# Recurrence of a test-time-training layer: corrections in two sets of matmuls, query products moved, no filler

## The chip, the cores and the metric

The kernel runs on one core of one Trainium2 chip. The metric is the device time of one execution in microseconds (us): the median of the runs, from the start of the execution to its end. Beside it stands one execution taken by the profiler, whose span runs from the first to the last instruction. A core has five engines with a queue each: PE (TensorE, matmuls into PSUM), DVE (VectorE), ACT (ScalarE), POOL (GpSimd) and SP (SyncE, which issues the DMAs here). They wait for each other by semaphores alone.

## The reference

Two residual layers follow each other on an image of 4 x 256 x 32 x 32. The second, a convolution with a spatial descriptor, is not touched by the change. The first is a layer whose state, a matrix W1 (32 x 32) and a bias b1 for each of 8 heads and 4 images, is trained while it reads: the 1024 tokens go through in 64 chunks of 16, and each chunk takes one gradient step. Its core:

```python
def _ln_l2_bwd(Z, tgt, g, b):
    D = Z.shape[-1]
    mu = Z.mean(-1, keepdims=True)
    var = ((Z - mu) ** 2).mean(-1, keepdims=True)
    std = jnp.sqrt(var + EPS_IN)
    xh = (Z - mu) / std
    gxh = (g * xh + b - tgt) * g
    return (D * gxh - gxh.sum(-1, keepdims=True) - xh * (gxh * xh).sum(-1, keepdims=True)) / (D * std)
...
def step(carry, inp):
    W1c, b1c = carry
    xq, xk, xv, et = inp
    Z1 = xk @ W1c + b1c
    grad = _ln_l2_bwd(Z1, xv - xk, g, bb)
    Attn1 = jnp.tril(xq @ xk.swapaxes(-1, -2))
    b1_bar = b1c - jnp.tril(et) @ grad
    Z1_bar = xq @ W1c - et * Attn1 @ grad + b1_bar
    last_eta = et[..., -1, :, None]
    W1n = W1c - (last_eta * xk).swapaxes(-1, -2) @ grad
    b1n = b1c - (last_eta * grad).sum(-2, keepdims=True)
    return ((W1n, b1n), xq + _ln(Z1_bar, g, bb, EPS_IN))
```

## The kernel before

**Stages.** Everything is float32. A first block normalises the input, a second makes queries, keys and values with their rotation (to about 160 us). The third block holds the scan over the 64 chunks (first start of a chunk's work on ACT at 168.3 us, last at 450.5 us), and behind it the output projection and the second layer. The change touches the scan alone.

**A chunk of the scan.** The 128 partitions are 4 groups of 32 rows; a group holds two heads with 16 tokens each, and the 4 images lie side by side in the free dimension, so a tile of one chunk is 128 x 128. Two buffers alternate by the chunk's parity `p`, with `o = 1 - p`.

- PE's `base` (L1157 to L1178) makes Z of the next chunk with the state as it stands, and in the same matmuls the products of keys with keys and of queries with keys: 16 matmuls of 64 rows (L1169), then one with the identity for the bias (L1175). All go to one PSUM bank, `ZB[p]`: per image 32 columns of Z and 32 of products. A float32 matmul is two records in the trace, so 16 matmuls are 32 records.
- That state lacks the gradient of the chunk just before. So the gradient `GL` of chunk c-1 is put into chunk c by a correction: `grads(ZW, ZB[p], o, 1)` (L1180 to L1189, matmuls at L1184) multiplies the masked products `AM` by `GL` and adds to Z in the same bank, 16 matmuls of 32 x 32.
- ACT squares the corrected Z (L1573). DVE sums the squares (L1317), sums and centres Z (L1318, L1322), and with standard deviation and variance from ACT and the rate from POOL makes the gradient in two terms: `YC` (L1353), from the target and its mean, and `WX` (L1355), the centred Z by a factor; `GL` is their sum (L1358). YC and GL lie in SBUF, WX in PSUM bank 7.
- With `GL` PE then makes the `update` of state (L1196) and bias (L1204), and `grads(HD, QB[o], o, 0)`, the attention's part of the chunk's output (L1184 again). ACT copies the state to SBUF (L1514, `wcopy`) and the bias (L1518, `bcopy`), and later in its list the products from the bank of Z to SBUF (L1548, semaphore `s1`); POOL masks these (L1428, `am`).
- The query part of the output, queries by state, is 16 matmuls of 64 rows (L1248) into bank `QB[p]`. DVE adds the bias and drains that bank (L1296, `zq`); the output's norm follows, two or more chunks later, in `out_var` (L1301), `out_turn` (L1311) and others.

**What sets the order.** Every engine's list is written out by hand and runs in its order; there is no scheduler. On PE the body of chunk c (L1214 to L1253) is: wait for `gl`, `am` and `s1`; correction; wait for `khx` and `bcopy`; update; attention of chunk c-1; a filler (L1211), one matmul of the identity by 256 columns of a table, whose result nobody reads; `base` of chunk c+1, which waits for `wcopy`; query of chunk c, which waits for `wcopy` and for the drain `zq`. PE alone runs a loop: 15 passes of four chunks (L1135), with two chunks written out ahead of it and two behind; the other engines' 64 chunks are written out. ACT's body (L1569 to L1600) is: square, two copies for outputs, standard deviation, variance, copies of state and bias, in chunks 40 to 47 one gain of 512 columns (L820), then `khx`, `qt2`, `next_k` (L1534), `products` (L1548) and the output's standard deviation.

The wait for `s1` ahead of the correction is there because ACT reads the products from the bank to which the correction writes.

## Time and profile before

| | |
|---|---|
| median of 3 runs | 584.75 us (584.35 to 589.26) |
| profiled execution, its own time | 586.26 us |
| its span, first to last instruction | 584.5 us |
| granted TensorE clock, mean over the span | 0.958 |
| PE busy | 479.3 us (82%), 12552 matmul records |
| DVE busy | 430.8 us (74%) |
| ACT busy | 346.9 us (59%) |
| POOL busy | 328.3 us (56%) |
| chain that ended last, by engine | PE 26%, DVE 26%, ACT 10%, issue 9%, POOL 1% |

A row of the timeline gives start and duration in us from the span's start, engine, line of the kernel, operation, what it writes and reads, and how many instructions it merges; in brackets stands the idle time of the engine just before, and who ended it by the semaphores. Instructions of one engine overlap a little: the next one's start often comes 0.1 us before the end shown for the one ahead. "PEld" is PE's load of weights. "issue" is waiting that no instruction in the profile explains. The granted clock is 1.00 at 2.4 GHz and 0.50 at 1.2 GHz.

### The profile page before, as it was taken

What the parts mean: (1) busy time and instruction counts of PE and PEld (TensorE: products, weight loads), DVE (VectorE), ACT (ScalarE), POOL (GpSimd) and SP (SyncE); (2) the same over time, 40 slices, a digit from 0 to 9 for tenths busy, and PEclk for the clock granted to TensorE, in tenths of its full rate; (3) what the DMA queues carried; (4) which work ended last, traced back from release to release, by engine and by line L of the source; (5) the groups of instructions that cost most, each with busy time, mean ns of one, the idle gap of its engine ahead of it and who ended that gap; (6) DMA issues with size and microseconds to landing.
All of it is one profiled execution on the core that took longest, in us unless ns stands there. A gap on an engine that the chain in (4) does not pass through costs nothing.

```text
span 584.5 us, 30359 instructions
## 1 busy us (share of the span) xinstructions
PE 479.3 (82%) x12552; PEld 311.6 (53%) x12552; DVE 430.8 (74%) x1516; ACT 346.9 (59%) x1165; POOL 328.3 (56%) x590
## 2 busy tenths in 40 slices
PE   0289988889558889888888888888897699998995
PEld 0144443334346667676767676667675244455662
DVE  5466888888746588888888988888885567676552
ACT  1255344322256588888888889988785477553320
POOL 1159888777734366666666655566763577330112
PEclk9999999999959799999999999999997799998998
DMA  8301111111100011111111000001010500000123
GB/s 337 121 0 37 36 37 36 38 36 36 38 18 23 21 28 37 27 36 28 36 28 36 1 1 1 19 36 37 19 36 4 170 1 1 1 2 1 73 74 144
DMA packets 15136, 24.74 MB, mean 42 GB/s; under 512 B 4228, under 2 KB 4968, under 8 KB 15080
## 3 DMA queue, kind: packets, MB, share of 16 engines
q1 hardware_dynamic: 15080, 24.10, 13.3%
q8 instruction: 23, 0.38, 0.3%
q14 instruction: 33, 0.27, 0.2%
HBM read 11.50 MB, written 4.19 MB: 27 GB/s over the span
## 4 chain that ended last, share of the span: by engine, by line
PE 26%; DVE 26%; ACT 10%; issue 9%; POOL 1%; POOLq 0%; ACTq 0%
PE PS L1184 6%; PE PS L941 4%; PE PS L1272 3%; ACT work L1573 3%; PE PS L923 3%; PE PS L427 3%; DVE work L1358 2%; DVE work L1353 2%; DVE work L1339 2%; DVE work L1317 2%; DVE work L1336 2%; DVE PS L1355 2%; DVE PS L1340 2%; DVE PS L1342 2%; DVE PS L1319 2%
## 5 line engine op out<-in xcount | busy, mean ns | idle before, releaser
L1184 PE MATMUL PS<-work 32*32 32x32 f32 x4064 | 60.4, 195 | 38.4 <-DVE work L1358 25.1
L1184 PEld LDWEIGHTS PS<-work 32*32 32x32 f32 x4064 | 54.5, 108 | 43.9 <-issue 43.7
L1428 POOL TENSOR_TENSOR work<-work,mask 128x256 f32<-128x256 f32 x64 | 46.8, 731 | 38.1 <-ACT work L1548 38.1
L575 PE MATMUL PS<-X,work 128*128 128x512 f32 x128 | 58.1, 598 | 0.4 <-ACT X L501 0.4
L1317 DVE TENSOR_REDUCE work<-work 128x4 f32<-128x128 f32 x64 | 18.3, 286 | 52.2 <-ACT work L1573 52.2
L1440 POOL TENSOR_TENSOR work<-work,lrh 128x4 f32<-128x4 f32 x64 | 13.0, 203 | 75.2 <-DVE work L1331 69.7
L694 POOL TENSOR_TENSOR work<-work 128x512 f32<-128x512 f32 x32 | 43.9, 1373 | 6.7 <-DVE work L637 6.1
L1169 PEld LDWEIGHTS PS<-work 64*32 64x32 f32 x2048 | 33.1, 111 | 25.7 <-issue 24.5
L1169 PE MATMUL PS<-work 64*32 64x64 f32 x2048 | 43.9, 226 | 3.5 <-issue 2.5
L1211 PE MATMUL PS<-cst 128*128 128x256 f32 x126 | 45.6, 444 | 0.0
L1525 ACT ACTIVATE work<-TK,small 128x128 f32<-128x128 f32 x128 | 44.3, 402 | 0.0
L1196 PE MATMUL PS<-work 32*64 32x32 f32 x2016 | 43.5, 224 | 0.7 <-issue 0.7
L1541 ACT ACTIVATE work<-QP,cst 128x128 f32<-128x128 f32 x128 | 43.9, 396 | 0.0
L1412 POOL TENSOR_TENSOR work<-KP,cst 128x256 f32<-128x256 f32 x64 | 39.3, 614 | 5.6 <-POOLq L519 5.6
L898 POOL TENSOR_TENSOR TK<-TK 128x512 f32<-128x512 f32 x7 | 8.9, 1293 | 53.1 <-ACT TK L1094 53.1
L1196 PEld LDWEIGHTS PS<-work 32*64 32x64 f32 x2016 | 36.4, 136 | 3.5 <-issue 0.9
L575 PEld LDWEIGHTS PS<-X,work 128*128 128x128 f32 x128 | 23.2, 190 | 25.8 <-issue 25.1
L636 DVE TENSOR_TENSOR work<-PS,work 128x512 f32<-128x512 f32 x32 | 21.7, 678 | 20.2 <-POOL KP L697 14.6
L1561 ACT ACTIVATE work<-work,small 128x4 f32<-128x4 f32 x64 | 18.9, 296 | 24.3 <-DVE work L1301 24.3
L1272 PE MATMUL PS<-TK,wsm 128*128 128x512 f32 x64 | 31.4, 616 | 1.6 <-ACT X L1617 1.6
L1175 PE MATMUL PS<-work,cst 128*128 128x128 f32 x128 | 32.5, 337 | 0.0
L1573 ACT ACTIVATE work<-PS 128x128 f32<-128x128 f32 x64 | 17.8, 277 | 23.1 <-PE PS L1184 19.6
(174 smaller groups left out, 1332.0 us busy)
## 6 DMA issues: line engine op xcount, KB each, us to landing
X<-in_x SPq DMA_DIRECT2D x4, 1024.0 KB, 8.2
TK<-KP SPq DMA_DIRECT2D x64, 64.0 KB, 1.9
X<-QP SPq DMA_DIRECT2D x64, 64.0 KB, 2.0
TK<-in_x SPq DMA_DIRECT2D x16, 256.0 KB, 2.9
out<-TK SPq DMA_DIRECT2D x16, 256.0 KB, 2.5
work<-in_rope SPq DMA_DIRECT2D x2, 512.0 KB, 9.2
cst<-in_consts SPq DMA_DIRECT2D x1, 289.0 KB, 5.1
work<-in_wk SPq DMA_DIRECT2D x1, 256.0 KB, 11.1
```

The costliest lines, as they stand in the source:

```text
L575: mm = nc.tensor.matmul(PS[:, 2 + m, :], lhs(j), xt(i, j), start=(j == 0), stop=(j == J - 1))
L694: nc.gpsimd.tensor_tensor(ksw[:, t, :], ksw[:, t, :], sinT[:, h], ALU.mult).then_inc(s_ksin, 1)
L1169: mm = nc.tensor.matmul(PS[HD * a:HD * a + HD, ZB[p], b * ZW:b * ZW + ZW], KT2[p][r:r + 64, k * B + b, :, :].rearrange("p e t -> p (e t)") ...
L1184: mm = nc.tensor.matmul(PS[HD * a:HD * a + HD, bank, b * width:b * width + HD], AM[p][HD * a:HD * a + HD, b, part, :, :].rearrange("p e t ...
L1196: mm = nc.tensor.matmul(PS[2 * HD * a2:2 * HD * a2 + 2 * HD, WB + k, b * HD:b * HD + HD], KHX[p][HD * a:HD * a + HD, b, :, :].rearrange("p ...
L1211: nc.tensor.matmul(PS[:, QB[p], 256:512], ident, ccol("spread", 0, 256), start=True, stop=True, skip_group_check=True)
L1272: mm = nc.tensor.matmul(PS[:, 2 + m, :], wsm[:, j, m * P:(m + 1) * P], ot(i, j), start=(j == 0), stop=(j == J - 1))
L1412: nc.gpsimd.tensor_tensor(KT2[p], chunk(KP, c).unsqueeze(2).broadcast_to([P, J * B, E, CS]), ccol("emask_k").unsqueeze(1).unsqueeze(3).bro ...
L1428: nc.gpsimd.tensor_tensor(AM[p].rearrange("p b s e t -> p (b s) e t"), S1[p].unsqueeze(2).broadcast_to([P, 2 * B, E, CS]), mask2.rearrange ...
L1525: kx = nc.scalar.activation(KHX[p][:, :, e, :].rearrange("p b (f t) -> p b f t", f=E), head_rows(1, c), ACT.Copy, scale=upd_mask[:, e:e + 1])
L1541: a = nc.scalar.activation(QT2[p][:, :, e, :], chunk(QP, c), ACT.Copy, scale=ccol("emask_k", e, 1))
L1573: nc.scalar.activation(SQ, zb, ACT.Square).then_inc(q["sq"], 1)
```

## The change

It has four parts. (1) PE's correction of a chunk is made in two sets of 16 matmuls, one with `YC` and one with `WX` as moving operand, and both add to the bank of Z; the first waits for `yc`, `am` and `s1`, the second for `w`. The semaphore `corr`, for which ACT's square waits, is raised by the second. `GL` is still made, for update and attention, and PE waits for `gl` ahead of the update. (2) On DVE, `out_var` of chunk c-2 stands ahead of the sum `GL`, and `WX` is a tile in SBUF instead of PSUM. (3) The query products of a chunk are no longer the last part of its body on PE: they stand in the next chunk's body, between update and attention, as `query_base`; the last chunk's stand behind the loop's last bodies. (4) The filler is gone.

```diff
-        TS, SQ, YL, YC = (carve(B, HD) for _ in range(4))
+        TS, SQ, YL, YC, WX = (carve(B, HD) for _ in range(5))
...
-        PZ, WX, ZC = (home(at) for at in range(3))
-        at = 3 * B * HD
+        PZ, ZC = (home(at) for at in range(2))
+        at = 2 * B * HD
...
-                def grads(width, bank, p, part):
+                def grads(width, bank, p, part, rows):
...
-                                                  GL[p][HD * a:HD * a + HD, b, :],
+                                                  rows[HD * a:HD * a + HD, b, :],
...
-                def filler(p):
-
-                    nc.tensor.matmul(PS[:, QB[p], 256:512], ident, ccol("spread", 0, 256), start=True, stop=True,
-                                     skip_group_check=True)
...
-                        pe.wait_ge(q["init"], 1)
-                        pe.wait_ge(q["gl"], done)
-                        pe.wait_ge(q["am"], done)
-                        pe.wait_ge(q["s1"], now)
-                        grads(ZW, ZB[p], o, 1).then_inc(q["corr"], 1)
-                        pe.wait_ge(q["init"], 1)
-                        pe.wait_ge(q["khx"], done)
-                        pe.wait_ge(q["bcopy"], done)
-                        update(o)
-                        grads(HD, QB[o], o, 0).then_inc(q["attn"], 1)
-                        if past(c, 2):
-                            pe.wait_ge(q["zq"], before)
-                        filler(p)
-                    else:
-                        base(0, 0, 1, 1)
-                    if not is_last(c):
-                        base(c + 1, o, nxt, now)
-                    else:
-                        pe_mean(pe, 0, True)
+                def query_base(ready, p, drained):
+
                     pe.wait_ge(q["init"], 1)
-                    pe.wait_ge(q["qt2"], now)
-                    pe.wait_ge(q["wcopy"], now)
-                    if past(c, 2):
-                        pe.wait_ge(q["zq"], before)
+                    pe.wait_ge(q["qt2"], ready)
+                    pe.wait_ge(q["wcopy"], ready)
+                    if drained is not None:
+                        pe.wait_ge(q["zq"], drained)
...
-                                    R[o][r:r + 64, k, b, 0:HD], start=(b == 0), stop=False,
+                                    R[1 - p][r:r + 64, k, b, 0:HD], start=(b == 0), stop=False,
...
+                    if past(c, 1):
+                        pe.wait_ge(q["init"], 1)
+                        pe.wait_ge(q["yc"], done)
+                        pe.wait_ge(q["am"], done)
+                        pe.wait_ge(q["s1"], now)
+                        grads(ZW, ZB[p], o, 1, YC)
+                        pe.wait_ge(q["init"], 1)
+                        pe.wait_ge(q["w"], done)
+                        grads(ZW, ZB[p], o, 1, WX).then_inc(q["corr"], 1)
+                        pe.wait_ge(q["init"], 1)
+                        pe.wait_ge(q["gl"], done)
+                        pe.wait_ge(q["khx"], done)
+                        pe.wait_ge(q["bcopy"], done)
+                        update(o)
+                        query_base(done, o, before)
+                        grads(HD, QB[o], o, 0, GL[o]).then_inc(q["attn"], 1)
+                    else:
+                        base(0, 0, 1, 1)
+                    if not is_last(c):
+                        base(c + 1, o, nxt, now)
+                    else:
+                        pe_mean(pe, 0, True)
...
                 run_chunks(pe, body)
+                query_base(NC, 1, NC - 1)
                 pe.wait_ge(q["gl"], NC)
                 pe.wait_ge(q["am"], NC)
-                grads(HD, QB[1], 1, 0).then_inc(q["attn"], 1)
+                grads(HD, QB[1], 1, 0, GL[1]).then_inc(q["attn"], 1)
...
                     nc.vector.tensor_tensor(WX, ZC, bc(cc1), ALU.mult).then_inc(q["w"], 1)
-                    dve.wait_ge(q["w"], c + 1)
                     dve.wait_ge(q["yc"], c + 1)
-                    nc.vector.tensor_tensor(GL[p], WX, YC, ALU.add).then_inc(q["gl"], 1)
-
                     if past(c, 2):
                         out_var(c - 2)
+                    dve.wait_ge(q["w"], c + 1)
+                    nc.vector.tensor_tensor(GL[p], WX, YC, ALU.add).then_inc(q["gl"], 1)
+
```

On PE, one chunk inside the loop (from the step of the loop's registers, L124, to the end of its body) reads as follows, rows of before with a minus and of after with a plus; L1220 is the query's line in the changed kernel:

```order
 L124 ISA
-L1184 MATMUL PS<-work 32x32 x16
+L1184 MATMUL PS<-work 32x32 x32
 L1196 MATMUL PS<-work 64x32 x16
 L1204 MATMUL PS<-work,ones_blk 32x128 x4
+L1220 MATMUL PS<-work 32x32 x16
 L1184 MATMUL PS<-work 32x32 x16
-L1211 MATMUL PS<-cst 128x256
 L1169 MATMUL PS<-work 32x64 x16
 L1175 MATMUL PS<-work,cst 128x4x32
-L1248 MATMUL PS<-work 32x32 x16
```

The correction ahead of the update has doubled to 32 matmuls, the query group has moved from the body's end to the place ahead of attention, and the filler between attention and `base` is left out.

On DVE, the end of a chunk's list in the middle of the scan before, with the semaphores waited for (scan_zn and scan_attn belong to the output's path):

```order
L1349 SCALAR_TENSOR_TENSOR work<-PS,work 128x4 [waits scan_u2,scan_m]
L1353 TENSOR_TENSOR work<-work,PS 128x128 [waits scan_cy,scan_yl]
L1355 TENSOR_TENSOR PS<-PS,work 128x128 [waits scan_c]
L1358 TENSOR_TENSOR work<-PS,work 128x128 [waits scan_yc,scan_w]
L1301 TENSOR_REDUCE work<-work 128x4 [waits scan_sqq]
L1311 STREAM_TRANSPOSE work<-work 128x128 [waits scan_zn]
L1296 TENSOR_TENSOR work<-PS,work 128x128 [waits scan_zn,scan_attn]
```

and the same place in the changed kernel, where the lines have moved by one to three:

```order
L1350 SCALAR_TENSOR_TENSOR work<-PS,work 128x4 [waits scan_u2,scan_m]
L1354 TENSOR_TENSOR work<-work,PS 128x128 [waits scan_cy,scan_yl]
L1356 TENSOR_TENSOR work<-PS,work 128x128 [waits scan_c]
L1302 TENSOR_REDUCE work<-work 128x4 [waits scan_sqq,scan_yc]
L1361 TENSOR_TENSOR work<-work 128x128 [waits scan_w]
L1312 STREAM_TRANSPOSE work<-work 128x128 [waits scan_zn]
L1297 TENSOR_TENSOR work<-PS,work 128x128 [waits scan_zn,scan_attn]
```

The reduction of `out_var` (L1301, now L1302) has moved between the product WX and the sum GL, and WX (L1356) is now written to SBUF.

## Rows read from the trace of the kernel before

**Rows 1.** ACT's square by its line: steady chunks, first pass, end of scan.

```profile
L1573 ACT ACTIVATE work<-PS x56: 277/278/278, 202.5 to 436.7; 128x128 f32<-128x128 f32 x56
...
L1573 ACT ACTIVATE work<-PS x5: 277/278/278, 179.2 to 202.5; 128x128 f32<-128x128 f32 x5
...
L1573 ACT ACTIVATE work<-PS x2: 278/278/278, 444.5 to 450.5; 128x128 f32<-128x128 f32 x2
```

**Rows 2.** Timeline of chunk 38; start and duration in us.

```profile
336.50 0.28 ACT L1573 ACTIVATE work<-PS 128x128 f32<-128x128 f32 x1 [0.50 <-PE PS L1184]
...
336.96 0.42 PE L1204 MATMUL PS<-work,ones_blk 32*32 32x128 f32 x8
...
337.52 0.42 ACT L1514 ACTIVATE work<-PS 128x128 f32<-128x128 f32 x2
...
337.60 0.70 PE L1211 MATMUL PS<-cst 128*128 128x256 f32 x2
...
338.23 0.65 PE L1169 MATMUL PS<-work 64*32 64x64 f32 x32
...
338.81 0.49 PE L1175 MATMUL PS<-work,cst 128*128 128x128 f32 x2
...
339.12 0.29 DVE L1353 TENSOR_TENSOR work<-work,PS 128x128 f32<-128x128 f32 x1
339.16 0.30 ACT L1534 ACTIVATE work<-KP 128x128 f32<-128x128 f32 x1
...
339.23 0.46 PE L1248 MATMUL PS<-work 64*32 64x32 f32 x32
339.33 0.29 DVE L1355 TENSOR_TENSOR PS<-PS,work 128x128 f32<-128x128 f32 x1
339.36 0.36 ACT L1548 ACTIVATE work<-PS,small 128x128 f32<-128x128 f32 x1
339.65 0.29 DVE L1358 TENSOR_TENSOR work<-PS,work 128x128 f32<-128x128 f32 x1
...
340.05 0.45 PE L1184 MATMUL PS<-work 32*32 32x32 f32 x32 [0.36 <-DVE work L1358]
...
340.28 0.26 DVE L1296 TENSOR_TENSOR work<-PS,work 128x128 f32<-128x128 f32 x1
...
340.43 0.67 PE L1196 MATMUL PS<-work 32*64 32x32 f32 x32
...
340.57 0.28 ACT L1573 ACTIVATE work<-PS 128x128 f32<-128x128 f32 x1
```

**Rows 3.** Timeline of chunk 43, one of the eight with a gain on ACT.

```profile
358.40 0.28 ACT L1573 ACTIVATE work<-PS 128x128 f32<-128x128 f32 x1 [0.48 <-PE PS L1184]
...
361.96 0.36 ACT L1548 ACTIVATE work<-PS,small 128x128 f32<-128x128 f32 x1
...
362.46 0.45 PE L1184 MATMUL PS<-work 32*32 32x32 f32 x32 [0.88 <-ACT work L1548]
...
362.98 0.28 ACT L1573 ACTIVATE work<-PS 128x128 f32<-128x128 f32 x1 [0.48 <-PE PS L1184]
```

**Rows 4.** Timeline of chunk 37, behind which PE's loop branches back.

```profile
332.03 0.28 ACT L1573 ACTIVATE work<-PS 128x128 f32<-128x128 f32 x1
...
335.98 0.45 PE L1184 MATMUL PS<-work 32*32 32x32 f32 x32 [0.76 <-DVE work L1358]
```

**Rows 5.** Timeline of chunk 57, in which POOL is late.

```profile
418.77 0.28 ACT L1573 ACTIVATE work<-PS 128x128 f32<-128x128 f32 x1
...
422.80 0.37 ACT L1548 ACTIVATE work<-PS,small 128x128 f32<-128x128 f32 x1 [1.07 <-PE PS L1175]
...
423.96 0.45 PE L1184 MATMUL PS<-work 32*32 32x32 f32 x32 [0.81 <-ACT work L1548]
```

**Rows 6.** Stretches: PE, PEld, DVE, ACT, POOL busy (instructions), clock, DMA share, GB/s.

```profile
201.00:439.80 238.80, 207.61 (x9652) 165.54 (x9642) 203.91 (x1003) 201.70 (x848) 151.11 (x394) 1.00 0.09 25
443.40:450.20 6.80, 6.18 (x179) 4.83 (x183) 3.65 (x18) 3.45 (x14) 1.13 (x4) 0.50 0.02 5
```

More of the change, by code:

```diff
@@ L1250, in body @@
                                     QT2[p][r:r + 64, k * B + b, :, :].rearrange("p e t -> p (e t)"),
-                                    R[o][r:r + 64, k, b, 0:HD], start=(b == 0), stop=False,
+                                    R[1 - p][r:r + 64, k, b, 0:HD], start=(b == 0), stop=False,
                                     skip_group_check=True)
                     mm.then_inc(q["qbase"], 1)
+                def body(c, p):
+                    o = 1 - p
+                    done, now, nxt = value(pe, c), value(pe, c + 1), value(pe, c + 2)
+                    before = value(pe, c - 1) if past(c, 2) else None
+                    if past(c, 1):
[20 more added lines that the diff above has]
+                        pe_mean(pe, 0, True)
                 run_chunks(pe, body)
+                query_base(NC, 1, NC - 1)
                 pe.wait_ge(q["gl"], NC)
                 pe.wait_ge(q["am"], NC)
-                grads(HD, QB[1], 1, 0).then_inc(q["attn"], 1)
+                grads(HD, QB[1], 1, 0, GL[1]).then_inc(q["attn"], 1)
                 def project(i, first):
```

5 lines of the change are left out of this document (removed).

## The prediction

> **What bounds the kernel now.** I read four views, in this order: one line's instructions, the timeline of one chunk, the same timeline where the chunk differs, and the clock by stretches. The square of the corrected Z on ACT (L1573) runs once per chunk, so its starts are the beat of the scan: from the seventh chunk to the 62nd there are 56 starts between 202.5 and 436.7 us, 55 intervals in 234.2 us, 4.26 us on average [rows 1]. What else the change touches lies before or behind that stretch and is short, so the question is what one interval is made of.
>
> The timeline of chunk 38 [rows 2] shows it; I count from its square at 336.50. DVE starts YC at 2.62, WX at 2.83, their sum GL at 3.15; PE's correction group (L1184, 32 records) starts at 3.55, its update follows 0.38 later, and the next square starts at 4.07, 0.52 after the group's start. So from GL's start to PE it takes 0.40 (0.29 of it the add), and GL itself starts 0.32 after WX. Beside this runs a second chain that is easily missed: ACT goes through its list and reaches the copy of the products (L1548) at 2.86. PE waits for that copy too (s1), because it reads the bank to which the corrections are added. In this chunk it comes early enough to stay unseen.
>
> In eight chunks it does not: there ACT also does a gain, the copy starts at 361.96, and PE's group at 362.46, named as waiting for L1548 and not for GL [rows 3]. That prices the wait: copy start plus 0.50; the interval is 4.58 instead of 4.07. For chunk 38 the same rule gives 2.86 + 0.50 = 3.36. **The slack of the second chain is 3.55 - 3.36 = 0.19 us, no more.**
>
> A third kind of chunk is the one behind which PE's loop branches back: the interval from 332.03 to 336.50 is 4.47, and the group starts at 335.98, 3.95 after its square [rows 4]. Of the 13 branches in the stretch ten show this; two fall among the gain chunks, which are later anyway, and one in chunk 57.
>
> **The two sets.** The sum of YC and WX no longer stands ahead of PE. By the 0.40 from DVE to PE, the YC set could start at 2.62 + 0.40 = 3.02 and the WX set at 3.23. But the first set writes the bank, so it now carries the wait for s1: 3.36, not 3.02. The WX set is 16 more matmuls, 32 records, behind it on the same engine; a group of this form takes 0.38 to the next one's start [rows 2]. So it starts at 3.36 + 0.38 = 3.74, and the next square comes 0.52 later, at 4.26, where GL's way gave 4.07. WX, ready for PE at 3.23, gains nothing by that. **An ordinary interval becomes 4.26, 0.19 longer**: the add goes from the path, and a group of 0.38 comes behind a wait that has 0.19 of slack.
>
> Can the copy come earlier? On ACT it stands behind next_k (2.66, and 0.20 to the next start), and it needs base's last matmul, which ends at 338.81 + 0.49, or 2.80 [rows 2]. Both allow 2.86; ACT's list is unchanged, so an earlier base buys nothing.
>
> **Filler and query.** Without the filler, base no longer stands behind it (0.63 from 337.60 to 338.23). The query group comes in ahead of attention: ones at 0.46, query 0.24 later as attention is now, then attention and base at 0.38 each, at most 1.46. Base also waits for the copy of the state, which ends at 1.02 + 0.42 = 1.44; with 0.14 to PE (the 0.50 above less that copy's 0.36) it starts at 1.58 instead of 1.73. Base ends 0.15 earlier, and the copy of the products does not move: 0. Attention is 0.38 later; DVE's out_rows, at 3.78, has over 2 us of room. The query's wait for zq is met by out_rows of the chunk before, which ends at 4.04 [rows 2], ahead of this square.
>
> **The branch.** Now the bias matmul of base is the last group of the loop, not the query. Before, the group behind the branch started 1.22 after the query's start (2.73 to 3.95) and 1.64 after the bias matmul's (2.31). The bias matmul is now at 2.16, so the bounds are 3.38 and 3.80. I take the early one, practically the 3.36 that s1 sets, since the branch stands behind the last instruction issued, and the query's 32 records are gone from there. So the ten intervals of 4.47 become 4.26, a gain of 2.1 us in all; at the late bound they would be 4.70, and the sum 4.4 us larger.
>
> **The DVE edits.** WX goes to SBUF instead of PSUM: YC, written to SBUF, takes 0.29, WX in PSUM 0.29 [rows 2]; between -0.02 and +0.02, and not on the path: 0. out_var stands before the add, which then starts at about 3.23 instead of 3.15; with 0.40 it reaches PE at 3.63, while update comes behind the WX set at 4.12: 0, covered by 0.49. If DVE's last instruction of the chunk, now ending at 4.04, kept its place or moved by less than 0.2, it would stay ahead of the next square.
>
> **The sum, 7th to 62nd chunk.** 46 intervals of 4.26 are 196.0. The eight gain chunks: copy start 3.56, first set 4.06, second 4.44, square 4.96 (before 4.58): 39.7. Chunk 57, where POOL is late: copy at 422.80, so first set 423.30, second 423.68, square 424.20, which is 5.4 from 418.77; before, PE's group stood at 423.96 [rows 5]. Together 241.1 against 234.2: **+6.9**.
>
> Ahead of that lies PE's first pass through its loop, four intervals from 179.2 to 202.5, 23.3 us where four average ones would take 17.0 [rows 1]: an excess of 6.3, in stalls of PE. The loop now has 404 matmuls for 344, so I let the excess grow by the same sixth, 1.1, and add 4 x 0.2: +2. Bounds: -1 (the longer interval hides part of the stalls) to +6 (the excess doubles). At the end the last query waits for the drain of chunk 62, which DVE finishes at about 4.0 of the last chunk, instead of running straight behind the mean's matmuls: +0.5, between 0 and 1. In all +9.4 us. That is a difference from the profiled execution, 586.26 us around its span of 584.5; the same difference on the median of the runs, 584.75, gives **594 us**.
>
> **Rivals.** *The products are no bound (not slower).* If ACT's copy started by 2.50 after the square, the WX set would start at 3.40 (behind a first set at 3.02) and the square come at 3.92: 0.15 less on 36 intervals and 0.55 on ten, -11 us, so 574 us. For it: GL is what PE is seen waiting for at the ends of ordinary chunks. Against it: between 2.66 and 2.86 ACT has no gap in which to gain 0.36, and rows 3 price the wait. It decides at a copy start of 2.67, where the interval is again 4.07. Chance 0.06.
>
> *The second set costs less.* If its matmuls overlap the first set's (0.20 in place of 0.38), the ordinary interval is 4.08, the ten branches still gain 0.39 each, the gain chunks lose 0.2 each: +0.4 - 3.9 + 1.6, with the start and the end +2.5, so 585 us. Against it: the two groups of this kind in rows 2 stand 0.38 apart. Chance 0.15, with other offsets that end within 1%.
>
> *The clock falls without the filler.* The filler is PE's longest block in a chunk but for base. The granted clock is 1.00 from 201 to 439.8, with PE 87% busy, and 0.50 (1.2 GHz) from 443.4 to 450.2 [rows 6], where PE comes from a stall; the interval there is 6.0 [rows 1]. My ordinary chunk leaves PE idle for 0.7 of 4.26 (2.65 to 3.36), the gain chunk for 1.4 of 4.96, against 0.9 of 4.58 now, at full clock [rows 3]. If half of the 55 intervals ran at 6.0: 27 x 1.7 = +46, about 640 us. Chance 0.06 for the whole; a few low stretches (two intervals each, +3 us) are in my range. The Trainium skill (TensorE: Matmul & The Clock Gate, A second HAM failure mode) says that short but frequent idling between groups of matmuls makes the clock swing between its levels. By that rule this case would be the likely one, near 640 us. The trace does not bear it out so far: such gaps stand in every chunk, at 1.00.
>
> *The loop's code no longer stays with PE.* Only the first pass shows the stalls; the other 14 run without. If each stalled as the first, at 7.4 us, that would be 14 x 7.4 = +104, about 698 us. Chance 0.04. The Trainium skill (Runtime: NRT & Kernel Launch, Instruction fetch mechanics) says that a taken branch to code outside the two-page window stops for a fetch; by that rule the present loop would stall in each pass, and rows 4 show 0.4 at a branch, not the microseconds of the first pass.
>
> **How the numbers follow.** My case with its terms has 0.69: 594, its own range 588 to 603 (the first pass -3 to +4, the branch +4.4, a low stretch or two +3, a tenth less for each set -2). Below it lie the two first rivals, above it clock and code. The range 588 to 606 leaves out the first rival, most of the second and the two dear ones, and takes in partial ones. A measurement of this kernel tells about 1% (5.8 us) from no change: slower 0.74, same 0.20, faster 0.06.
>
> **What would show it.** In the profile after: the first of two L1184 groups waiting for the copy of the products in every ordinary chunk; next_k to copy still 0.20 apart, the copy at 2.86; square to square 4.26, also behind the branch; gain chunks near 4.96; WX long done when the second set starts; granted clock 1.00 through the scan. I am wrong if the group waits for YC or WX, if the interval is at or below 4.07, if the branch still shows (4.7), or if stretches of low clock appear.

## The result, and the profile after

| | before | after |
|---|---|---|
| median of 4 runs beside each other | 585.63 us | **619.55 us** (614.17 to 622.73) |
| ratio, 95% interval | | 1.0594, 1.0539 to 1.0648 |
| profiled execution, its span | 586.26, 584.5 us | 619.98, 618.2 us |
| granted clock, mean | 0.958 | 0.864 |
| chain that ended last | PE 26%, DVE 26%, ACT 10% | PE 41%, ACT 24%, issue 5%, DVE 3% |

Slower, as forecast, but by 34 us instead of 9, and outside the range of 588 to 606. Ratios leave out executions more than 1.5% above the fastest of the same kernel; where the clock spreads a kernel's executions that is up to three of four (E13), so their range is given too.

From the page of the changed kernel: the granted clock in 40 slices, the queue that fetches instructions, and PE's corrections as a group (busy us, mean ns, idle before and its releaser).

```profile
PEclk9999999999555556999999977889855689999898
...
q8 instruction: 25, 0.41, 0.3%
...
L1184 PE MATMUL PS<-work 32*32 32x32 f32 x6080 | 87.3, 207 | 47.6 <-ACT work L1549 40.9
```

The first line has three dips that the kernel before does not have in this size. The last says that PE's corrections now wait for the copy of the products (L1549, formerly L1548), 40.9 of 47.6 us, and no more for GL: the mechanism of the forecast. The squares by their line answer to [rows 1] (the line is now L1574), in the same order.

```profile
L1574 ACT ACTIVATE work<-PS x56: 277/278/279, 206.9 to 464.9; 128x128 f32<-128x128 f32 x56
...
L1574 ACT ACTIVATE work<-PS x5: 277/278/278, 179.0 to 206.9; 128x128 f32<-128x128 f32 x5
...
L1574 ACT ACTIVATE work<-PS x2: 278/278/278, 474.2 to 481.2; 128x128 f32<-128x128 f32 x2
```

The 55 intervals take 258.0 us in place of 234.2: +23.8. The first pass takes 27.9 in place of 23.3: +4.6. From the 62nd square to the end of the span it is 153.3 (618.2 - 464.9) in place of 147.8: +5.5. Ahead of the third square nothing changed (179.0 and 179.2). The sum, +33.7, is the whole difference of the spans.

Chunk 38, the one of [rows 2], with the square of the chunk ahead of it, behind which the loop branches back:

```profile
347.21 0.28 ACT L1574 ACTIVATE work<-PS 128x128 f32<-128x128 f32 x1 [0.52 <-PE PS L1184]
...
351.36 0.28 ACT L1574 ACTIVATE work<-PS 128x128 f32<-128x128 f32 x1 [0.52 <-PE PS L1184]
...
353.02 0.65 PE L1169 MATMUL PS<-work 64*32 64x64 f32 x32
...
353.60 0.49 PE L1175 MATMUL PS<-work,cst 128*128 128x128 f32 x2
...
353.98 0.29 DVE L1354 TENSOR_TENSOR work<-work,PS 128x128 f32<-128x128 f32 x1
354.02 0.30 ACT L1535 ACTIVATE work<-KP 128x128 f32<-128x128 f32 x1
354.19 0.28 DVE L1356 TENSOR_TENSOR work<-PS,work 128x128 f32<-128x128 f32 x1
354.22 0.36 ACT L1549 ACTIVATE work<-PS,small 128x128 f32<-128x128 f32 x1
...
354.58 0.28 DVE L1361 TENSOR_TENSOR work<-work 128x128 f32<-128x128 f32 x1
...
354.73 0.74 PE L1184 MATMUL PS<-work 32*32 32x32 f32 x64 [0.64 <-ACT work L1549]
...
355.44 0.67 PE L1196 MATMUL PS<-work 32*64 32x32 f32 x32
355.51 0.28 ACT L1574 ACTIVATE work<-PS 128x128 f32<-128x128 f32 x1 [0.52 <-PE PS L1184]
```

Counted from the square at 351.36: next_k 2.66, copy 2.86, corrections 3.37. The forecast had 2.66, 2.86 and 3.36. WX starts at 2.83 and is done long before PE comes to it. Both sets are one group of 64 records, 0.74 long, and the next square starts at 4.15, not 4.26. Behind the branch it is 4.15 too (347.21 to 351.36). So at full clock a chunk costs 0.08 more than the 4.07 of before. That cannot make 23.8 us; the clock does. Stretches of the scan, columns as in [rows 6]:

```profile
156.40:241.70 85.30, 68.47 (x2296) 54.45 (x2296) 47.30 (x215) 44.84 (x177) 31.84 (x83) 0.50 0.08 20
241.70:364.60 122.90, 102.48 (x5932) 84.10 (x5935) 104.07 (x522) 103.50 (x439) 79.39 (x205) 1.00 0.10 25
364.60:405.50 40.90, 34.64 (x1552) 27.83 (x1548) 28.37 (x144) 32.37 (x125) 20.30 (x55) 0.75 0.04 13
405.50:443.10 37.60, 30.64 (x1785) 25.06 (x1785) 30.95 (x155) 31.57 (x135) 25.63 (x62) 1.00 0.09 29
443.10:487.40 44.30, 37.50 (x1216) 28.39 (x1216) 23.04 (x117) 21.67 (x89) 18.06 (x45) 0.50 0.10 29
```

PE runs at 0.50 to 241.7 us (before: to 201, with a break from 177.1 to 194.2), swings between 0.50 and 1.00 in the gain chunks, and falls again at 443.1. What a chunk looks like at 0.50 (chunk 8):

```profile
219.12 0.28 ACT L1574 ACTIVATE work<-PS 128x128 f32<-128x128 f32 x1 [1.09 <-PE PS L1184]
...
222.75 0.79 PE L1175 MATMUL PS<-work,cst 128*128 128x128 f32 x2
223.58 0.37 ACT L1549 ACTIVATE work<-PS,small 128x128 f32<-128x128 f32 x1 [1.22 <-PE PS L1175]
...
224.09 1.08 PE L1184 MATMUL PS<-work 32*32 32x32 f32 x64 [0.55 <-ACT work L1549]
...
225.23 0.28 ACT L1574 ACTIVATE work<-PS 128x128 f32<-128x128 f32 x1 [1.10 <-PE PS L1184]
```

It lasts 6.11. PE is now what everybody waits for: ACT waits 1.22 for the end of base, and yet PE itself waits 0.55 for the copy that follows base. Chunk 43, with the gain, at full clock, beside [rows 3]:

```profile
376.33 0.28 ACT L1574 ACTIVATE work<-PS 128x128 f32<-128x128 f32 x1 [0.75 <-PE PS L1184]
...
380.40 0.74 PE L1184 MATMUL PS<-work 32*32 32x32 f32 x64 [1.36 <-ACT work L1549]
...
381.19 0.28 ACT L1574 ACTIVATE work<-PS 128x128 f32<-128x128 f32 x1 [0.74 <-PE PS L1184]
```

The interval is 4.86, and PE waits 1.36 for the copy.

### The profile page after: what moved, and what is told of

Same layout as the page of the kernel before. It is cut to its first block, busy times and chain, and to the rows that moved or that the text cites. A ratio compares the mean times of both kernels' runs of the same rounds, so it can differ in the third digit from the quotient of the medians.

```text
span 618.2 us, 34266 instructions
## 1 busy us (share of the span) xinstructions
PE 505.9 (82%) x14442; PEld 335.4 (54%) x14442; DVE 425.2 (69%) x1516; ACT 349.7 (57%) x1165; POOL 330.5 (53%) x590
## 3 DMA queue, kind: packets, MB, share of 16 engines
HBM read 11.50 MB, written 4.19 MB: 25 GB/s over the span
## 4 chain that ended last, share of the span: by engine, by line
PE 41%; ACT 24%; issue 5%; DVE 3%; POOL 0%; POOLq 0%; ACTq 0%
PE PS L1184 11%; ACT work L1542 4%; PE PS L1169 4%; ACT work L1549 4%; ACT work L1526 4%; PE PS L1196 4%; PE PS L941 3%; PE PS L427 3%; PE PS L1273 3%; PE PS L1175 3%; PE PS L923 3%; ACT work L1515 2%; PE PS L1220 2%; PE PS L1204 2%; ACT work L1574 2%
## 5 line engine op out<-in xcount | busy, mean ns | idle before, releaser
L1184 PE MATMUL PS<-work 32*32 32x32 f32 x6080 | 87.3, 207 | 47.6 <-ACT work L1549 40.9
L1184 PEld LDWEIGHTS PS<-work 32*32 32x32 f32 x6080 | 73.6, 119 | 63.7 <-issue 60.6
L1429 POOL TENSOR_TENSOR work<-work,mask 128x256 f32<-128x256 f32 x64 | 48.7, 761 | 63.4 <-ACT work L1549 63.4
L1169 PE MATMUL PS<-work 64*32 64x64 f32 x2048 | 52.3, 253 | 2.1 <-issue 1.2
L1196 PE MATMUL PS<-work 32*64 32x32 f32 x2016 | 50.2, 241 | 0.5 <-DVE work L1361 0.3
L1196 PEld LDWEIGHTS PS<-work 32*64 32x64 f32 x2016 | 43.9, 157 | 4.2 <-issue 0.8
L1574 ACT ACTIVATE work<-PS 128x128 f32<-128x128 f32 x64 | 17.8, 277 | 48.7 <-PE PS L1184 48.7
L1169 PEld LDWEIGHTS PS<-work 64*32 64x32 f32 x2048 | 39.9, 128 | 5.9 <-issue 1.7
L1549 ACT ACTIVATE work<-PS,small 128x128 f32<-128x128 f32 x64 | 23.2, 363 | 28.4 <-PE PS L1175 28.4
L1175 PE MATMUL PS<-work,cst 128*128 128x128 f32 x128 | 38.4, 390 | 0.0
L1220 PEld LDWEIGHTS PS<-work 64*32 64x32 f32 x2048 | 26.0, 122 | 18.7 <-issue 18.7
L1220 PE MATMUL PS<-work 64*32 64x32 f32 x2048 | 33.8, 211 | 0.4 <-issue 0.4
```

The costliest lines, as they stand in the source:

```text
L1169: mm = nc.tensor.matmul(PS[HD * a:HD * a + HD, ZB[p], b * ZW:b * ZW + ZW], KT2[p][r:r + 64, k * B + b, :, :].rearrange("p e t -> p (e t)") ...
L1175: nc.tensor.matmul(PS[:, ZB[p], 0:B * ZW].rearrange("p (b n) -> p b n", b=B)[:, :, 0:HD], ident, Bs[1 - p if past(n, 1) else 0], start=Fal ...
L1184: mm = nc.tensor.matmul(PS[HD * a:HD * a + HD, bank, b * width:b * width + HD], AM[p][HD * a:HD * a + HD, b, part, :, :].rearrange("p e t ...
L1196: mm = nc.tensor.matmul(PS[2 * HD * a2:2 * HD * a2 + 2 * HD, WB + k, b * HD:b * HD + HD], KHX[p][HD * a:HD * a + HD, b, :, :].rearrange("p ...
L1220: mm = nc.tensor.matmul(PS[HD * a:HD * a + HD, QB[p], b * HD:b * HD + HD], QT2[p][r:r + 64, k * B + b, :, :].rearrange("p e t -> p (e t)") ...
L1429: nc.gpsimd.tensor_tensor(AM[p].rearrange("p b s e t -> p (b s) e t"), S1[p].unsqueeze(2).broadcast_to([P, 2 * B, E, CS]), mask2.rearrange ...
```

## The experiments

The theory to be tested: the filler's absence lets PE's clock fall, and this is most of the loss. The rivals: the two sets cost more than their length; moving the query costs; the longer code does. Short names: E1 to E14 in the order in which they ran. The times of before beside them were 583.4 to 586.2 us.

**E1: the changed kernel with a filler again**, behind base, where PE waits for the copy.

```diff
                         base(c + 1, o, nxt, now)
+                        if past(c, 1):
+                            filler(p)
```

> The changed kernel with the filler put back, but behind base, in the wait for the products' copy. Theory (the loss beyond the sets comes from the clock, and the clock from the missing filler): granted clock 1.00 through the loop's steady passes, ordinary interval 4.15 us as in the changed kernel's own stretches at full clock, gain interval 4.86, no interval of 6.1; about 588 us. Rival (the two sets with the longer code of the loop keep PE at the low clock, filler or not): long stretches at 0.50 remain, above 610 us. If the filler does not fit into the gap of 0.66 us, the interval grows to 4.3 or more and the time to 596.

Measured: 596.20 us, ratio 1.0196 (1.0154 to 1.0239). One stretch and one chunk of it:

```profile
205.50:447.80 242.30, 220.10 (x11373) 172.70 (x11367) 201.04 (x1008) 201.81 (x847) 153.50 (x394) 1.00 0.09 25
```

```profile
266.26 0.60 PE L1211 MATMUL PS<-cst 128*128 128x256 f32 x2
...
266.56 0.36 ACT L1556 ACTIVATE work<-PS,small 128x128 f32<-128x128 f32 x1
...
267.06 0.74 PE L1184 MATMUL PS<-work 32*32 32x32 f32 x64 [0.21 <-ACT work L1556]
...
267.85 0.28 ACT L1581 ACTIVATE work<-PS 128x128 f32<-128x128 f32 x1 [0.52 <-PE PS L1184]
```

The clock is 1.00 from 205.5 to 447.8, the interval still 4.15: the filler lies wholly in PE's wait and costs nothing there. 619.55 - 596.20 = **23.4 us are the missing filler's**. The 55 intervals now take 235.6 us, +1.4 on before. The rest of E1's +7.8 in its profiled execution is the first pass (+4.1), the end (+3.5) and an earlier start (-1.3). So the theory holds for the clock and for every interval, while the time is 8 above the 588 it gave. That it equals the last case's 596 is chance: the filler did fit.

**E2: the kernel before, without its filler** and nothing else changed.

```diff
-                        if past(c, 2):
-                            pe.wait_ge(q["zq"], before)
-                        filler(p)
```

> The kernel before without its filler, nothing else. Theory: PE's list gets a gap behind attention and the clock falls in some stretches, as in the changed kernel: intervals near 6 us there, 600 to 620 us. Rival (sets and query move, not the filler, bring the low clock): the clock stays at 1.00, the interval at 4.07, and base, 0.15 earlier, lets the branch cost a little less: 583 us.

Measured: 608.38 us (599.23 to 611.46), ratio 1.0314 (1.0224 to 1.0403), mean clock 0.827 in the profiled execution. Two stretches, and PE's two waits in an ordinary chunk of the second:

```profile
252.50:307.10 54.60, 53.38 (x1832) 45.74 (x1832) 40.23 (x198) 39.82 (x164) 28.13 (x76) 0.50 0.11 27
...
331.00:361.70 30.70, 22.75 (x1249) 19.41 (x1240) 25.55 (x126) 25.45 (x108) 19.26 (x50) 1.00 0.02 5
```

```profile
350.48 0.65 PE L1169 MATMUL PS<-work 64*32 64x64 f32 x32 [0.42 <-ACT work L1511]
...
352.43 0.45 PE L1184 MATMUL PS<-work 32*32 32x32 f32 x32 [0.50 <-DVE work L1355]
```

The filler alone, in an otherwise unchanged kernel, is worth 23 us by the medians (14 to 26 by the single executions). The first row also corrects the theory: at 0.50 PE is busy 53.38 of 54.60 us, with hardly a wait, and the clock does not come back for 54 us. A wait cannot be all that holds it down. Nor does it take a gain chunk to bring it down: here it fell in ordinary chunks, at 252.5 and 313.9, where PE at full clock waits 0.42 ahead of base and 0.50 ahead of the corrections.

**E3: the two sets alone**: filler, query and DVE's order stay as before, WX lies in SBUF.

```diff
-                        pe.wait_ge(q["gl"], done)
+                        pe.wait_ge(q["yc"], done)
...
-                        grads(ZW, ZB[p], o, 1).then_inc(q["corr"], 1)
+                        grads(ZW, ZB[p], o, 1, YC)
+                        pe.wait_ge(q["init"], 1)
+                        pe.wait_ge(q["w"], done)
+                        grads(ZW, ZB[p], o, 1, WX).then_inc(q["corr"], 1)
```

> The kernel before with the correction in two sets and WX in SBUF; query, filler and DVE's order as before. Theory: interval = products' copy at 2.86, plus 0.50, plus 0.79 for both sets to the square, 4.15 in ordinary chunks, 4.86 in gain chunks, and behind a branch 3.95 + 0.79 = 4.74; clock 1.00 as before. 36 x 0.08 + 10 x 0.27 + 8 x 0.28 = +8 us, about 594 us. Rival (the sets by themselves are what lowers the clock): stretches at 0.50, above 605 us.

Measured: 602.12 us, ratio 1.0304 (1.0264 to 1.0344). Clock 1.00 from 214.4 to 463.6. Ordinary intervals 4.19 to 4.22, but 4.83 behind the branch, where the changed kernel and E1 have 4.15. So the query move is what hides the branch, and the two sets without it pay 0.6 at each; the filler's absence does not hide it, since E2, without filler and with the query last, still has 4.38 there for 4.06. The 55 intervals take 247.0 us; the first six, 39.2 against 34.2, are as long as E1's 38.8, so that loss does not come from the query move. The rival falls, as the clock stays; the time is 8 above the expected 594.

**E4: the query move alone**: one set on GL, DVE's order as before, and the filler behind the attention as before.

```diff
                         update(o)
-                        grads(HD, QB[o], o, 0).then_inc(q["attn"], 1)
-                        if past(c, 2):
-                            pe.wait_ge(q["zq"], before)
+                        query_base(done, o, before)
+                        grads(HD, QB[o], o, 0, GL[o]).then_inc(q["attn"], 1)
                         filler(p)
```

> The kernel before with the query moved ahead of attention, one set with GL, the filler kept behind attention (WX in SBUF). Theory: base now stands behind query and filler, starts at about 2.06 instead of 1.73 and ends at 3.13, so the copy comes at 3.19 and not at 2.86, PE's group at 3.69 instead of 3.55: ordinary interval 4.21; the branch is hidden (10 x 0.25 less); gain chunks as before. 36 x 0.14 - 10 x 0.26 = +2 us, about 587 us, clock 1.00. Rival (the query's move costs nothing and gains the branch): interval 4.07, 580 us.

Measured: 738.84 us (683.48 to 741.10). A clear miss, and the largest loss but one of the study. The profile, by one stretch and one chunk:

```profile
196.30:605.90 409.60, 373.32 (x10134) 269.24 (x10126) 216.19 (x1064) 219.91 (x888) 158.80 (x414) 0.50 0.07 19
```

```profile
302.26 1.22 PE L1211 MATMUL PS<-cst 128*128 128x256 f32 x2
...
304.42 0.80 PE L1175 MATMUL PS<-work,cst 128*128 128x128 f32 x2
305.25 0.37 ACT L1551 ACTIVATE work<-PS,small 128x128 f32<-128x128 f32 x1 [2.38 <-PE PS L1175]
...
305.77 0.65 PE L1184 MATMUL PS<-work 32*32 32x32 f32 x32 [0.55 <-ACT work L1551]
```

The filler is there in every chunk and the clock is 0.50 for 409.6 us. At 0.50 the filler takes 1.22 and stands ahead of base, base ends late, the copy comes after base, and the corrections after the copy: the interval is 6.83, and PE waits 0.55 in it. In this order of PE's list the filler does not keep the clock, and it makes the low state dearer. The place alone is not it: in the kernel before, the filler stood between attention and base too, at a clock of 1.00, but with the query behind base.

**E5: E4 with the filler behind base**, a single edit.

```diff
                         grads(HD, QB[o], o, 0, GL[o]).then_inc(q["attn"], 1)
-                        filler(p)
...
                         base(c + 1, o, nxt, now)
+                        if past(c, 1):
+                            filler(p)
```

> The run before this one with a single edit: the filler goes from behind the attention's corrections to behind the base; one set of corrections on GL, query products ahead of the attention, as there. Theory A (the clock is held by what stands between the base and the next corrections, since that is where PE waits for the products' copy): clock 1.00 from about 205 us to past the last loop pass; the corrections wait for GL as in the kernel before (group at 3.55, square at 4.07), the loop's branch is hidden behind the filler (4.07 there too, before 4.47), so the steady stage is 234.2 - 13 x 0.40 = 229 us and the time 580 to 587, by how long the first pass is. Rival B (moving the query products is itself what costs, by the base ending later): clock stays at 0.50 as in the run with the filler behind the attention, intervals of 6 us and more, time above 640.

Measured: 587.08 us, ratio 1.0020 (0.9982 to 1.0057).

```profile
220.20:442.10 221.90, 191.88 (x9138) 147.94 (x9134) 194.85 (x956) 191.61 (x806) 143.38 (x375) 1.00 0.09 25
```

The same matmuls, but for one filler fewer, in another order: 738.84 to 587.08 us. Intervals 4.05, behind the branch too, 4.58 in the gain chunks. Rival B falls: the query move, with the filler behind base, costs nothing that can be measured.

**E6: E1 with the second set issued twice.** The second term counts twice, so the output is not the reference's.

```diff
-                        grads(ZW, ZB[p], o, 1, WX).then_inc(q["corr"], 1)
+                        grads(ZW, ZB[p], o, 1, WX)
+                        grads(ZW, ZB[p], o, 1, WX).then_inc(q["corr"], 1)
```

> The changed kernel with the filler behind the base and the second set issued twice: the second term of the gradient is counted twice in the corrections, and nothing else differs. Theory A (a set that follows one of its own form costs 0.29, as read between 4.15 and the first set's end): ordinary interval 4.15 + 0.29 = 4.44, gain intervals 5.15, the square still the last wait; steady stage 235.6 + 55 x 0.29 = 251.5, time 596.2 + 61 x 0.29 = 614 plus up to 3 for a first pass at half clock. Rival B (the prediction's 0.38 from the group's whole length): 4.53, steady stage 256.5, time 619 and more. If PE's longer busy stretch also shortens the low clock of the first pass, up to 5 us less by either.

Measured: 859.60 us, ratio 1.4592 (1.4471 to 1.4713). Neither theory; the question was answered by E11 instead. From the page, the instruction queue and PE's corrections; then three rows of one chunk:

```profile
q8 instruction: 153, 2.51, 1.2%
...
L1184 PE MATMUL PS<-work 32*32 32x32 f32 x8096 | 141.8, 227 | 118.5 <-issue 114.3
```

```profile
353.23 1.06 PE L1211 MATMUL PS<-cst 128*128 128x256 f32 x2
356.50 0.87 PE L1184 MATMUL PS<-work 32*32 32x32 f32 x49 [2.21 <-issue]
358.69 0.86 PE L1184 MATMUL PS<-work 32*32 32x32 f32 x47 [1.32 <-issue]
```

The fetch queue moved 153 packets where the changed kernel has 25, PE stands 114.3 us ahead of corrections with nothing to wait for, and intervals are 7 to 12 us in every pass. The loop's branch itself, by its minimum, median and maximum in ns, takes 3.7 us (median), where E1's takes 0.22:

```profile
L1135 PEldq COMPARE_BRANCH  x15: 87/3717/4497, 209.5 to 707.4; - x15
```

This is the fourth rival of the prediction, "the loop's code no longer stays with PE", met one step further on: with 17 more matmuls per chunk than the changed kernel, the third set and the filler. By the Trainium skill (Runtime: NRT & Kernel Launch, Instruction fetch mechanics) a taken branch whose target is outside the current two-page window stops for a fetch. The trace agrees at E6's branch; other stalls of E6, as in the rows above, lie inside a pass. The changed kernel's loop, 404 matmuls a pass for E6's 472, ran without such stalls after its first pass. E6's loss is not fetching alone, since its mean clock fell to 0.729 as well.

**E7: E1 with the gain of chunks 40 to 47 behind the products' copy** (the same lines moved down in ACT's body, ahead of `out_sd`).

```diff
-                    if GAIN_AT <= c < GAIN_AT + B * J:
...
                         products(c + 1, 1 - p)
+                    if GAIN_AT <= c < GAIN_AT + B * J:
```

> The changed kernel with the filler behind the base and, in chunks 40 to 47, the gain of the output norm behind the products' copy on ACT and no longer ahead of the masked keys. Theory A (ACT's row up to the products' copy bounds the interval, the gain's 0.71 stands in it): those eight intervals 4.15 to 4.25 in place of 4.86, the steady stage 235.6 - 8 x 0.65 = 230.4, time 596.2 - 5.2 = 591. Rival B (the gain now delays the next square and the sqrt behind it): 4.5 or more there, time 593.5 to 596.

Measured: 590.94 us, ratio 1.0046 (1.0008 to 1.0085): 5.3 less than E1 by the medians. The eight intervals are 4.15 to 4.17 in place of 4.86. Theory A holds in its size: the copy's place in ACT's list is the bound.

**E8: E5 with the gain moved in the same way.**

> The run with one set and the filler behind the base, and the gain behind the products' copy as well. Theory A: gain intervals 4.07 in place of 4.58 or 4.6, so 8 x 0.5 = 4 us less than that run: 576 to 583, below both the kernel before and the changed one. Rival B (the clock falls or the first pass is as long as in the changed kernel with filler, 39 us in place of 34): 582 to 588, no gain on the kernel before.

Measured: **581.82 us, ratio 0.9946 (0.9905 to 0.9988)**, the one version of the whole kernel whose interval lies below 1, by half a per cent on before. From chunk 9 to chunk 60 its intervals are 4.05 or 4.06 but for five longer ones, the gain chunks' included, as theory A has it.

**E9: the kernel before with the filler at the end of the chunk's list, behind the query, and the gain moved.** Here the filler, which starts a new sum, comes between the query products and the attention that is added to them in the same bank, and the output is no longer the reference's; the work of a chunk is the same.

> The kernel before with two moves: the filler from behind the attention to behind the query products, the last row of the chunk on PE, and the gain of chunks 40 to 47 behind the products' copy on ACT. Nothing of the changed kernel is in it. Theory A (PE has 0.4 to spare before the group at 3.55, GL bounds; whatever stands last before it both keeps the clock and hides the loop's branch): ordinary interval 4.07, behind the branch 4.07 in place of 4.47, gain 4.07 in place of 4.58; first pass 34 us as before, since no row is longer; 585.4 - 5.4 - 4.2 = 576, between 574 and 580. Rival B (the filler between attention and base is what the clock needs, or the first pass lengthens as in the run with one set): 581 to 590, clock under 0.94.

Measured: 585.46 us, ratio 1.0021 (0.9988 to 1.0053). A miss by 9 us. The intervals are 4.13, not 4.07: the filler starts at 2.97, and the corrections, next on PE, at 3.60 instead of 3.55. And the branch still shows (4.34 to 4.49). In E5, where it is hidden, the last group starts at 2.49; that this is the reason fits, but was not tried.

**E10: E1 with half the filler**, 128 columns for 256.

> The changed kernel with a filler of 128 columns in place of 256 behind the base, so about half the filler's 0.6 us. Ordinary interval 4.15 wherever the clock is 1.00, as the filler lies in PE's wait for the copy in either case. Theory A (a wait of some 0.2 to 0.4 before the corrections, as the kernel before has 0.36 there, still lets the clock stand): 594 to 599, as with the whole filler. Rival B (the whole wait has to be filled): clock 0.50 for a good part of the scan, as in the changed kernel, 605 to 622.

Measured: 600.87 us, ratio 1.0235 (1.0174 to 1.0297). Between the two, nearer to A: interval 4.15, clock 1.00 from 213.5 to 431.9 but for 3.4 us among the gain chunks, where PE's wait is longest. It is 4.7 us above E1 by the medians, but the two ratios' intervals overlap.

**E11: E1 with the first set alone.** The second term is left out of the corrections, so the output is not the reference's.

```diff
-                        grads(ZW, ZB[p], o, 1, YC)
-                        pe.wait_ge(q["init"], 1)
-                        pe.wait_ge(q["w"], done)
-                        grads(ZW, ZB[p], o, 1, WX).then_inc(q["corr"], 1)
+                        grads(ZW, ZB[p], o, 1, YC).then_inc(q["corr"], 1)
```

> The changed kernel with the filler behind the base and the first set of corrections alone: the second term of the gradient is left out of the corrections (not of the update and the attention). The first set starts at 3.37 behind the products' copy as with two; Theory A (the second set adds 0.29): square at 4.15 - 0.29 = 3.86, gain intervals 4.57; steady stage 235.6 - 55 x 0.29 = 219.7, time 578 or, with a first pass as short as before, 574. Rival B (0.38, the step of the prediction): square at 3.77, time 573 or 569. Rival C (another wait, GL's update or DVE's chain, ends at 4.0 or later, so that the second set cost less than its length): square at 4.0 or later, time 586 or more.

Measured: 579.08 us, ratio 0.9897 (0.9851 to 0.9942).

```profile
261.34 0.36 ACT L1553 ACTIVATE work<-PS,small 128x128 f32<-128x128 f32 x1
...
261.85 0.45 PE L1184 MATMUL PS<-work 32*32 32x32 f32 x32 [0.27 <-ACT work L1553]
...
262.37 0.28 ACT L1578 ACTIVATE work<-PS 128x128 f32<-128x128 f32 x1 [0.25 <-PE PS L1184]
```

Corrections 0.51 behind the copy's start, square 0.52 behind the corrections, interval 3.88. The second set costs 4.15 - 3.88 = **0.27**. Theory A, to 0.02. The records of the changed kernel say the same directly: of the 64 in a group, the 33rd starts 0.26 behind the first.

**E12: the kernel before with the gain moved**, nothing else.

> The kernel before with one move: the gain of chunks 40 to 47 behind the products' copy on ACT. Theory A (only ACT's row ahead of the copy bounds those eight chunks): their intervals 4.07, and 4.47 behind the branch, in place of 4.59; 8 x 0.52 - 2 x 0.40 = 3.4 us less, time 582.2, the first pass and all else as before. Rival B (the run with the gain moved in the one-set kernel gained 5 us by something else, a longer stretch at full clock): no change that can be measured, 584 to 587.

Measured: 585.53 us, ratio 0.9961 (0.9916 to 1.0007). Gain intervals 4.06, behind the branch 4.47 to 4.53, as expected; 3 us are too little for this measurement.

**E13: the changed kernel, no filler, with the gain moved**, and **E14: E1 with the filler in one of the loop's four chunks**. They ask what brings the clock down and what lifts it.

> The changed kernel without any filler, with the gain of chunks 40 to 47 behind the products' copy on ACT. In the changed kernel the clock stood at 1.00 for 123 us of ordinary chunks, in which PE waits 0.66 for the copy, and first fell in the gain chunks, where it waits 1.36. Theory A (the long wait of the gain chunks is what brings the clock down there): with waits of 0.66 in all of them 1.00 from some 240 to past 440 us; the low intervals and the 0.71 of the gain go, 13 us less: about 607. Rival B (the 0.66 alone lets the clock fall, and the place was chance): low stretches at other places of the scan, 610 to 625. The low first 85 us of the scan stay by either, since nothing is changed there.

> The changed kernel with the filler behind the base in one of the loop's four chunks only (3, 7, 11 and so on; one of the eight gain chunks in four too). Theory A (a chunk without a wait on PE is what lifts the clock, and one now and then is enough): the clock rises by some 215 us and stays to the gain chunks, of which some run low: 598 to 606. Rival B (each chunk needs it): low to 240 us as in the changed kernel, 612 to 620.

E13: 629.56 us (609.42 to 646.17), ratio 1.0783 (1.0679 to 1.0888), and the mean granted clock of its four executions is 0.88 to 0.73, so how long the low state lasts is left to chance there. The profiled one, of 609.42:

```profile
159.90:272.60 112.70, 96.02 (x3306) 76.77 (x3306) 62.58 (x302) 63.04 (x252) 44.99 (x118) 0.50 0.08 20
272.60:463.70 191.10, 158.19 (x9114) 129.67 (x9114) 161.61 (x810) 163.49 (x684) 125.39 (x320) 1.00 0.09 24
```

Once up, the clock stood at 1.00 for 191.1 us through the gain chunks, with waits of 0.66 in each chunk and no filler; in the changed kernel it fell there, with waits of 1.36. In that execution theory A holds; its time as a kernel does not, for the low stretch at the start got longer. E14: 607.16 us, ratio 1.0385 (1.0293 to 1.0476).

```profile
158.30:216.30 58.00, 46.24 (x1491) 36.70 (x1492) 30.90 (x140) 30.12 (x117) 21.19 (x55) 0.50 0.07 18
...
356.30:393.80 37.50, 33.09 (x1321) 26.61 (x1314) 24.45 (x125) 28.63 (x108) 17.18 (x46) 0.64 0.03 8
```

One filler in four chunks had the clock up at 216.3, where all had it at 205.5 and none at 241.7 and 272.6; among the gain chunks it falls. Half of the gain comes with a quarter of the fillers.

**What these kernels say of the clock together.** Each falls to 0.50 as the scan starts, at 156 to 162 us. The longest low stretch of each scan, one profiled execution per kernel:

| kernel | filler | PE's wait for the copy in a low chunk | longest low stretch, us |
|---|---|---|---|
| changed, E13 | none | 0.55 | 85.3, 112.7 |
| E2 | none | none | 54.6 |
| E4 | ahead of base | 0.55 | 409.6 |
| E1, E5 | behind base | none | 20.5, 30.7 |

The stretches of E1 and E5 lie at the start of the scan and in the loop's first pass, where PE also has stalls of its own. With the filler and without a wait in the low chunk the clock came back soon; with one of the two alone it stayed low longer. That is a pattern of these profiles, not a mechanism that they show. Downward, the clock fell with the long wait of the gain chunks twice (changed kernel, E14), and without that wait it stayed up there (E13, one profile); but in E2 it fell in ordinary chunks, and in E4 in the first pass, at 196.3. Why a nearly gapless PE stays at 0.50 in E2 no run here shows.

## Why the prediction was wrong

By its own steps, first the sum, in us of the profiled executions:

| stretch | predicted | changed kernel | E1, clock kept |
|---|---|---|---|
| to the third square | 0 | -0.2 | -1.3 |
| first pass | +2 | +4.6 | +4.1 |
| 55 intervals | +6.9 | +23.8 | +1.4 |
| from there to the end | +0.5 | +5.5 | +3.5 |

- **Failed: "Filler and query", priced at 0.** It counted the filler as 0.63 of PE's time ahead of base, and that part is right: base starts at 1.66 of the chunk for 1.58 forecast, and the copy stays at 2.86. It did not count what the filler does for the clock: 23.4 us by E1, 23 by E2. That was written down as the rival "the clock falls without the filler", with a chance of 0.06 and a price near 640. It was the case.
- **Why the rival got so little.** The argument against it was that such gaps stand in every chunk at a clock of 1.00. They were shorter there, 0.36 in an ordinary chunk and 0.88 in a gain chunk, and those chunks had the filler, so they could not speak for chunks without it. The idle times were predicted well (0.7 and 1.4 against 0.66 and 1.36); the conclusion was not theirs to give. The Trainium skill (TensorE: Matmul & The Clock Gate, A second HAM failure mode) said that short, frequent idling makes the clock swing. The trace agrees in the gain chunks, between 364.6 and 405.5, at a mean of 0.75, and E2 agrees in ordinary chunks; the changed kernel's ordinary chunks do not, where one wait of 0.66 in each left 1.00 for 122.9 us. The rival's own size, 27 slow intervals, was too large for this stretch: some 15 of the 55 were slow.
- **Mis-sized: the second set at 0.38.** It costs 0.27 (E11), 0.29 by the group's length (0.74 against 0.45). The 0.38 of rows 2 is the distance from a correction group to the update, whose matmuls have another form (32*64 weights for 32*32), though the forecast called the two groups of one kind; to a second set of the same form it is 0.26, so some 0.1 belongs to the change of form. With 0.11 less on 46 intervals, 5 of the 6.9 go; the gain chunks' 0.8 goes the same way, and 1 is left of the measured +1.4. The rival of the overlapping sets, 0.20, was off by 0.07 on the other side.
- **Right: the second chain.** The copy of the products at 2.86, corrections at copy plus 0.51, WX done long before. E7 and E11 confirm that the copy is the bound.
- **Right: the branch.** Hidden at 4.15 as at the early bound; E3 shows 4.83 where the query stays last, and in E5, where it is moved with one set, the branch is hidden too.
- **Right: the DVE edits.** GL starts at 3.22 and the update at 4.08: no wait.
- **Right in kind: gain chunks** 4.86 at full clock for 4.96 (the set's size again), and chunk 57, 5.3 in E1 for 5.4.
- **First pass +4.6 for +2**, inside its bounds (-1 to +6), but for another reason than the forecast's. It took the excess for stalls of PE. In the changed kernel the whole pass ran at 0.50, and four chunks of 6.11 are 24.4 of its 27.9. In E9's profile, at 1.00 from 177.9 on, the pass took 19.0 where before, with the clock at 0.50 from 194.2 to 201, it took 23.3. So the low clock makes most of the excess, and that the number fell inside the bounds is luck. With filler it is +4.1 (E1), with the query left last +3.3 (E3), with one set +1.4 to +1.9 (E5, E8, E11), so the second set has a part in it.
- **The end: +3.5 to +5.5 for +0.5**, outside its bounds of 0 to 1. The last query was counted, the clock from 443.1 on was not; what the other 3.5 are was not tried. One profile does not settle it: E5 and E8, alike in this stretch, have 149.5 and 145.8.

With the clock kept, the step list would have given 594 against E1's 596.2, by two errors that cancel, which is luck: the sets too dear, the first pass and the end too cheap.

## What to carry to other kernels

An instruction whose result nobody reads may still be what holds TensorE's clock: before it is removed, it has to be priced as if the clock could fall, and rows taken with it in place don't show what happens without it. Where it stands can matter more than that it stands: with the query moved and one set, the same matmul ahead of base and behind it made 739 and 587 us. And two independent terms into PE pay only if the engine's other wait leaves room; here 0.19 of slack stood against a set of 0.27.

## What the runs showed that was not expected

- PE can be busy 53.38 of 54.60 us at 0.50 without the clock rising (E2).
- A set of corrections behind one of its own form starts 0.26 after it, a group of another form 0.38 after it.
- Sixteen more matmuls per chunk (E6) turn a loop that is fetched once into one that is fetched in each pass: 25 packets to 153, and +263 us on E1, at a mean clock of 0.729.
- In two of the kernels without a filler behind base the time itself spreads: 609 to 646 us in E13, 683 to 741 in E4, where E1 has 594 to 598.
